# Whole rows per slot, roots in nine operations, and a new order of the first stage's lists in a routed FFN kernel

## The reference, cut to what matters

```python
# x: (128, 32, 256), 4096 tokens of 256
xc = einsum('bct,bcd->bdt', x, cond_weights[itok])        # one 32x32 matrix per batch
scores = sigmoid(xc @ gate_w.T)                            # 32 experts in 4 groups of 8
sb = scores + gate_bias
# best 2 groups by the sum of their 2 best sb, then the best 8 experts within them
wsel = scores[topi] / scores[topi].sum(-1) * 2.5           # cw: (4096, 32), zero elsewhere
x_lat = xc @ fc1_w.T                                       # 128 wide
h = relu2(x_lat @ w1[e].T) * cw[:, e]                      # relu2 is the square of relu
y_lat = sum over e of h @ w2[e].T
out = x + relu2(xc @ shared_up_w.T) @ shared_down_w.T + y_lat @ fc2_w.T
```

## Time and profile before

| | us |
|---|---|
| median of 3 runs | 442.08 |
| lowest, highest | 438.94, 444.67 |
| the profiled execution | 445.29 |
| its span, first to last instruction | 443.5 |

### The profile page before, as it was taken

The page is one execution under the profiler, slowest core; times in us unless marked ns, Lnnn a source line. Parts: engine busy times, 40 slices in busy tenths (PEclk is TensorE's granted clock), DMA queues, the critical chain, the costliest instruction groups (busy, mean ns, idle before and its releaser), DMA issues. The chain is left out here.

```text
span 443.5 us, 7029 instructions
## 1 busy us (share of the span) xinstructions
PE 397.0 (90%) x2261; PEld 345.9 (78%) x2261; DVE 307.5 (69%) x580; ACT 253.5 (57%) x330; POOL 197.5 (45%) x153
## 2 busy tenths in 40 slices
PE   8798989999989928799999999999999999999920
PEld 8788989999979828588888888888878888888810
DVE  0167997799898823697787887787767888876200
ACT  1274442734654520768778778778776787775310
POOL 5000076746776700006444576552644455434562
PEclk9899996999999968999999999999999999999555
DMA  6991473742752778858999988899998899979532
GB/s 173 251 308 41 144 289 102 239 177 72 239 220 96 223 226 257 261 181 225 210 222 234 200 214 231 222 216 315 329 351 224 231 209 304 358 221 243 111 40 31
DMA packets 66249, 93.55 MB, mean 211 GB/s; under 512 B 19295, under 2 KB 48086, under 8 KB 65622
## 3 DMA queue, kind: packets, MB, share of 16 engines
q1 hardware_dynamic: 52210, 77.71, 54.6%
q0 software_dynamic: 13296, 15.08, 20.1%
q10 hardware_dynamic: 708, 0.32, 0.3%
HBM read 94.48 MB, written 30.18 MB: 281 GB/s over the span
## 5 line engine op out<-in xcount | busy, mean ns | idle before, releaser
L530 POOL DMA_INDIRECT out_x<-res,sid_sb x70 | 122.0, 1742 | 161.9 <-DMA out_x<-res,sid_sb 72.0
L1011 DVE TENSOR_TENSOR act_lo<-act_full,act_hi 128x1024 fp32r<-128x1024 f32 (+3 forms) x92 | 105.9, 1151 | 24.7 <-ACT act_full L874 18.5
L1277 DVE SCALAR_TENSOR_TENSOR scaled<-h_banks,cond_bd 128x1024 f32<-128x1024 f32 (+3 forms) x76 | 86.5, 1138 | 42.3 <-PE h_banks L694 42.0
L694 PE MATMUL h_banks<-xc_hi,w_ring 128*128 128x512 f32 (+3 forms) x304 | 95.4, 396 | 4.0 <-DMA w_ring<-w_dram 1.8
L509 POOL DMA_INDIRECT rows_dram<-payload,slot_idx x64 | 68.6, 1072 | 56.0 <-DVE payload L1152 30.6
L715 PE MATMUL y_banks<-act_hi,w_ring 128*128 128x512 f32 (+3 forms) x304 | 79.3, 384 | 1.5 <-ACT act_hi L872 1.5
L872 ACT ACTIVATE act_hi<-scaled 128x1024 fp32r<-128x1024 f32 (+3 forms) x76 | 74.9, 986 | 2.6 <-PE y_banks L715 1.8
L874 ACT ACTIVATE act_full<-scaled 128x1024 f32<-128x1024 f32 (+3 forms) x76 | 74.7, 983 | 0.0
L715 PEld LDWEIGHTS y_banks<-act_hi,w_ring 128*128 128x128 f32 x304 | 56.7, 195 | 12.5 <-ACT act_hi L872 1.2
L694 PEld LDWEIGHTS h_banks<-xc_hi,w_ring 128*128 128x128 f32 x304 | 52.0, 193 | 16.1 <-issue 4.9
L694 PE MATMUL h_banks<-xc_lo,w_ring 128*128 128x512 f32 (+3 forms) x152 | 57.9, 381 | 0.0
(11 more groups left out here) (147 smaller groups left out, 642.3 us busy)
## 6 DMA issues: line engine op xcount, KB each, us to landing
w_ring<-w_dram SPq DMA_DIRECT2D x76, 512.0 KB
cond_bd<-s_dram SPq DMA_DIRECT2D x64, 512.0 KB, 5.5
w_dram<-w_ring SPq DMA_DIRECT2D x8, 1024.0 KB, 7.4
x_in<-in_x SPq DMA_DIRECT2D x8, 512.0 KB, 6.8
res<-in_experts_raw SPq DMA_DIRECT2D x4, 1024.0 KB, 10.2
out_x<-x_in SPq DMA_DIRECT2D x8, 512.0 KB, 3.8
rows_sb<-rows_dram SPq DMA_DIRECT2D x16, 256.0 KB, 4.8
rows_dram<-in_pad_rows SPq DMA_DIRECT2D x5, 328.0 KB, 4.3
```

Of the source, the lines that this page charges most:

```text
L530: pool.indirect_dma_start(out, bass.IndirectOffsetOnAxis(ap=sid_sb[:, i % SID_RING, j, GROUP_SIZE:PER_GROUP], axis=0), res[:, i % 2, j * H ...
L694: last = pe.matmul(h_banks[:, s, m * BANK:m * BANK + SIZE[i]], w, v, start=n == 0, stop=n == 2)
L1011: dve.tensor_tensor(lo, full, hi.bitcast(f32), ALU.subtract).then_inc(act_lo_ready, 1)
L1277: dve.scalar_tensor_tensor(pair(scaled, i, u), h, 0.0, scale, ALU.max, ALU.mult).then_inc(scaled_ready, 1)
```

## The change

- Row layout: a row is now 128 latents, 32 roots and one id (161 words for 164). SP loads a whole row per slot, `load_rows(i)` only, into a ring of eight tiles that lies in `payload`; `sid_sb`, `rows_sb` and the table's column are gone. The routing's scratch gets a tile of its own.
- ACT gets `gather_s(i)`: it copies all 32 roots of a tile's rows into `s_rows`; PE transposes 128 columns instead of 36, `store_s` writes 128 rows of 512 B instead of 36, and `load_scale` picks the group by the table.
- `roots` has nine operations: one step of second and one of third order from another start.
- `scatter` has no pauses.
- SP: `store_shared(3)` and (4) ahead of `store_split(2)`; `store_split(3)` behind the first two row loads; rows are loaded four tiles ahead.
- The lists of PE, ACT and DVE in the first stage are put in another order.

```diff
-ROW = LAT + GROUPS * PER_GROUP
+ID = LAT + EXPERTS
+ROW = ID + 1
...
             def load_rows(i):
+                row_of.append(sp.value_load(table[0:1, T_ROW + i:T_ROW + i + 1], min_val=0, max_val=DUMMY))
+                if i >= ROWS_RING:
+                    sp.wait_ge(out_added, ADDS_TO[i - ROWS_RING + 1] * DMA)
+                src = rows_dram[bass.ds(row_of[i], SIZE[i]), :].rearrange("(p j) c -> p j c", j=ROWS_OF[i])
+                sp.dma_start(tile_rows[:, i % ROWS_RING, 0:ROWS_OF[i], :], src)\
+                    .then_inc(rows_loaded[i % ROWS_RING], DMA)
...
-                src = s_dram[i % S_RING, 2 * u * SIZE[i]:(2 * u + 2) * SIZE[i]].rearrange("(a n) -> a n", a=1)
+                of_group = s_dram[i % S_RING, 0:EXPERTS * SIZE[i]].rearrange("(g n) -> g n", g=GROUPS)
+                src = of_group[bass.ds(group_of[i], 1), 2 * u * SIZE[i]:(2 * u + 2) * SIZE[i]]
...
             for u in range(PAIRS):
                 load_weights(0, u)
-            store_split(3)
             sp.wait_ge(pads_stored, GROUPS * DMA)
             sp.wait_ge(dummy_stored, DMA)
             sp.wait_ge(rows_scattered, scatters(BATCHES - 1))
-            load_sid(0)
             load_rows(0)
-            read_table(1)
-            load_sid(1)
             load_rows(1)
+            store_split(3)
             store_shared(6)
...
-                    if n == FIRST_TILE[k] + BT and k < 2:
-                        pool.wait_ge(rows_scattered, TOP_GROUPS * n * DMA)
...
+            def gather_s(i):
+                act.wait_ge(rows_loaded[i % ROWS_RING], (i // ROWS_RING + 1) * DMA)
+                if i >= 2:
+                    act.wait_ge(s_transposed, i - 1)
+                act.activation(s_rows[:, i % 2, 0:ROWS_OF[i], :], tile_rows[:, i % ROWS_RING, 0:ROWS_OF[i], LAT:ID],
+                               ACT.Copy).then_inc(s_rows_ready, 1)
...
+                c, y, q = (t[:, 0:NT[k], :] for t in (clamped, root, squared))
+                step(dve.tensor_scalar(c, cw[:, 0:NT[k], :], TINY, None, ALU.max))
+                step(dve.tensor_scalar(y.bitcast(i32), c.bitcast(i32), -0.5, INVERSE_ROOT, ALU.mult, ALU.add))
+                step(dve.tensor_tensor(q, y, y, ALU.mult))
+                step(dve.scalar_tensor_tensor(q, q, -STEP_LESS * 3 / 8, c, ALU.mult, ALU.mult))
+                step(dve.scalar_tensor_tensor(y, q, STEP_ALL * 3 / 8, y, ALU.add, ALU.mult))
+                step(dve.tensor_tensor(c, cw[:, 0:NT[k], :], y, ALU.mult))
+                step(dve.scalar_tensor_tensor(q, c, 64 / 9, y, ALU.mult, ALU.mult))
+                step(dve.scalar_tensor_tensor(q, q, -10 / 3, q, ALU.add, ALU.mult))
+                dve.scalar_tensor_tensor(payload[:, tiles_of(k), LAT:ID], q, 5.0, c, ALU.add, ALU.mult)\
+                    .then_inc(s_ready, 1)
```

More of the change, by code:

```diff
@@ L88 @@
 TABLE_CONSTS = INDEX0 + GROUPS
-T_ROW, T_GROUP, T_COL, T_NEED = (n * X_TILES for n in range(4))
-T_PAD = 4 * X_TILES
+T_ROW, T_GROUP, T_NEED = (n * X_TILES for n in range(3))
+T_PAD = 3 * X_TILES
 TABLE = T_PAD + GROUPS
@@ L132, in adaln_ffn @@
         act_lo = sb("act_lo", [P, 2, UNIT], f32r)
-        rows_sb = sb("rows_sb", [P, 2, BT, LAT])
-        sid_sb = sb("sid_sb", [P, SID_RING, BT, PER_GROUP], i32)
+        routing = sb("routing", [P, 4, NB * EXPERTS])
+        s_rows = sb("s_rows", [P, 2, BT, EXPERTS])
         s_t = sb("s_t", [P, 2, BANK])
@@ L155, in adaln_ffn @@
         biased, work, masked, left = (
-            rows_sb[:, n // 2, 2 * (n % 2):2 * (n % 2) + 2, :].rearrange("q j l -> q (j l)")
-            .rearrange("q (n e) -> q n e", e=EXPERTS) for n in range(4))
+            routing[:, n, :].rearrange("q (n e) -> q n e", e=EXPERTS) for n in range(4))
         cw, clamped, root, squared = (s_t[:, n // 2, (n % 2) * NB * EXPERTS:(n % 2 + 1) * NB * EXPERTS]
@@ L522, in _ @@
             for i in range(X_TILES):
[L523 removed]
+                pool.wait_ge(rows_loaded[i % ROWS_RING], (i // ROWS_RING + 1) * DMA)
                 if i > 0:
@@ L753, in _ @@
             project(5)
+            rank(1)
             shared_down(3)
-            rank(1)
             gate_and_latent(4)
@@ L762, in _ @@
             shared_up(6)
+            rank(2)
             shared_down(5)
-            gate_and_latent(6)
             shared_up(7)
             project(7)
-            rank(2)
+            gate_and_latent(6)
             shared_down(6)
@@ L770, in _ @@
             shared_up(8)
+            rank(3)
             shared_down(7)
-            rank(3)
             shared_up(9)
             shared_down(8)
+            rank(4)
+            count_all()
             shared_up(10)
@@ L777, in _ @@
             shared_up(11)
-            rank(4)
-            count_all()
             shared_down(10)
@@ L956, in _ @@
             square_shared(11)
-            for u in range(12, SHARED_UNITS):
-                relu_shared(u)
-                square_shared(u)
+            relu_shared(12)
+            square_shared(12)
+            relu_shared(13)
+            square_shared(13)
+            round_weights(3)
+            relu_shared(14)
+            square_shared(14)
+            relu_shared(15)
+            square_shared(15)
+            gather_s(0)
             copy_s(0)
@@ L964, in _ @@
             for i in range(1, 3):
+                gather_s(i)
                 copy_s(i)
@@ L973, in _ @@
                     round_x(i + 1)
+                if i + 3 < X_TILES:
+                    gather_s(i + 3)
                 square(i, 2)
@@ L1303, in _ @@
             slot_of_token(0)
+            combine_weights(0)
+            roots(0)
             rest_of_projection(3)
-            combine_weights(0)
             add_shared(0)
             rest_of_weights(0)
-            roots(0)
             rest(2)
@@ L1327, in _ @@
             pick_groups(2)
+            rest(6)
+            read_rank(2)
+            slot_of_token(2)
             largest(2)
             mark(2)
-            rest(6)
             add_shared(2)
@@ L1339, in _ @@
             pick_groups(3)
-            rest_of_weights(2)
-            add_shared(3)
-            rest(8)
-            read_rank(3)
-            slot_of_token(3)
             largest(3)
@@ L1348, in _ @@
             roots(3)
+            read_rank(3)
+            slot_of_token(3)
+            group_scores(4)
+            rest(8)
+            add_shared(3)
+            pick_groups(4)
+            largest(4)
+            mark(4)
             rest(9)
-            group_scores(4)
-            pick_groups(4)
-            add_shared(4)
-            rest(10)
             read_rank(4)
             slot_of_token(4)
-            largest(4)
-            mark(4)
-            rest(11)
             combine_weights(4)
             roots(4)
+            rest(10)
+            add_shared(4)
+            rest_of_weights(2)
+            rest(11)
             add_shared(5)
+            tile_table()
             rest(12)
-            tile_table()
             rest(13)
+            add_shared(6)
             rest_of_weights(3)
-            add_shared(6)
             rest(14)
```

110 lines of the change are left out of this document (36 added, 74 removed).

## The result

The changed kernel took 451.73 us (median of 4 runs, 449.19 to 453.58), the kernel before beside it 442.66 (438.94 to 444.67): a ratio of 1.0249, 95% interval 1.0183 to 1.0315. The quotient of the two medians is 1.0205; ratios here go by each kernel's fast runs, those within 1.5% of its fastest, so they can differ from that quotient (most of all for g3_mended, where two of ten runs count). The forecast was 439.2 with a range from 428 to 450. The profiled execution took 453.58 us, its span 451.7 us, 8.2 more than before.

The account below looks back on a forecast made before the run. It saw the kernel bound by the border between stages, DVE's list order in the first stage, and POOL's last adds. +3.7 us at the second stage's start and -6.5 at the end gave about -2.9, so 439.2 us, range 428 to 450.

Parts of the forecast that it names:

- Up to shared_up(6): First stage, PE: earlier rest(3) and rank(1) remove waits and the clock stays up, -5.3 us (bounds -2.0 to -5.3).
- To shared_down(8): First stage, from shared_up(6): DVE's list takes 32.0 us against PE's 27.2 of work, so PE waits, +4.8 us (0 to +6).
- To the end of shared_down(11): First stage, from shared_down(8): a 1.3 us wait for a rest behind roots(3) goes, -1.3 us (-1.3 to 0).
- tile_table ahead of rest(12): First stage, DVE: the table block delays shared_down(12), a 5.0 us PE wait, +4.4 us (+2 to +5).
- The clock: PE, first stage: of the two new waits, one counted as a fall to the low clock, +2.5 us (0 to +5).
- The border: Between stages: first scale transpose comes 3.7 us after PE's last unit instead of 7.8, -4.1 us.
- From the transpose to the experts: First scale transpose to first expert square: whole-row load of tile 2 and smaller terms, +2.7 us (0 to +5).
- The small terms of that sum: Transpose to experts: gather on ACT +0.4, one table read and issue fewer -0.7, last split meeting the scales' store +1.0 us.
- Second stage: Expert tiles: gathers, wider transposes and stores hide under PE's work, 0; without that cover 5.7 us.
- The end: Tail, POOL's adds into out: landings 0.8 us shorter over 8 tiles, -6.5 us (0 to -9).
- the two bad rivals meeting: Costlier lists (0.16) and no tail gain (0.20) together: 451.5 us; slower than 450.9 given chance 0.10.
- the rival in the prediction: Tail: adds don't land sooner, their own read and write setting the time; tail gives 0, 445.7 us, chance 0.20.

Follow-up runs that it names:

- g3_mended: Changed kernel with three moves of orders (table, rank reads, row loads) and a pause after every four tiles of scatters: 0.9701 of the kernel before, 463 kind.
- m1: Changed kernel, no pauses, rest(12) ahead of the table, rest(8) and add_shared(3) ahead of rank reads, row loads 2 and 3 earlier: 440.39 us, 0.9944, 443 kind.
- h1: Changed kernel with scales broadcast to partitions 0 to 63 alone, so outputs are not the reference's: 1.0118 of the kernel before, 443 kind.
- m2: Changed kernel with the three moves of orders and the kernel before's two pauses in the first two batches' scatters: 441.94 us, 1.0015, 443 kind.
- after_again: Changed kernel once more, nothing edited, on a chip of the 463 kind: 1.0432 of the kernel before.
- f3_pauses: Changed kernel with the pauses between the scatters of the first two batches put back: 1.0176 of the kernel before, 463 kind.
- e1: Changed kernel with rest(12) put back ahead of tile_table() in DVE's order: 1.0159 of the kernel before, 463 kind.
- e3: Changed kernel with row loads of tiles 2 and 3 right behind tile 1's on SP's queue: 1.0272 of the kernel before, 463 kind.
- g1: Changed kernel with a pause after every four tiles of scatters in all batches: 0.9991 of the kernel before, 463 kind.

## Why the prediction was wrong

By its own steps, span against span. The forecast was -2.8, the change +8.2.

- *Up to shared_up(6)*, -5.3: from shared_down(1) on -5.6, and the clock stayed up. Right. But shared_down(1) itself began 2.1 us later, behind a wait of 3.2 us and a shared_down(0) at a mean clock of 0.63 (36.96 to 41.50). The forecast had nothing for this. m1, with the same start, ran it at 36.56 in 3.10 us, so I take the 2.1 for a difference between executions; there is one profile of the changed kernel on this kind of chip.
- *To shared_down(8)*, +4.8: measured +5.4, with the 4.5 us wait on `x_in`. Right.
- *To the end of shared_down(11)*, -1.3 and with the clock's 2.5 +1.2: +1.5. Right.
- *tile_table ahead of rest(12)*, +4.4: the wait of 5.0 us came, and with the clock's price behind it the stretch took +6.2. Right.
- *The clock*, "I count one fall ... +2.5": wrong. Both new waits were followed by a stretch at the low clock, 121.0 to 126.4 at 0.50 and 153.0 to 158.1 at 0.55. The prediction had the rule of the Trainium skill before it ("TensorE: Matmul & The Clock Gate", on HAM oscillation), by which both fall; the trace agrees with it, and my middle between none and two had no ground.
- *The border*, -4.1: 164.52 to 169.84 is +5.3 on a PE that was 9.7 late, -4.4. Right, and 3.35 us of idle for 3.7.
- *From the transpose to the experts*, +2.7 (0 to +5): by the first copy of results +3.9. The cause I named, the whole-row load of tile 2 behind the weights, is the main one: in m1, where that load goes first, this stretch is only 0.5 us longer than before (35.1 for 34.6). The small terms of that sum (+0.4, -0.7, +1.0) rest on no row, and no run measured them one by one.
- *Second stage*, 0: -0.8 up to the 28th copy, with most of the gathers in it. Right.
- *The end*, "a sixth off a landing ... -6.5": this step failed, and it is the largest. A landing took 6.0 us for 5.8, and the tail 62.7 for 62.9. This is no accident of one execution: the tail took 61.4 to 68.7 us in the 14 profiles with whole rows (h1 aside) and 58.6 to 63.1 in the five with the old layout. The sign that I had named for it, a POOL wait total still near 72 us, reads 61.4 and would have misled: with the waits called "issue" the total is 104.7 us, and it was 102.2 before. The longest of the latter (in the kernel before 7.17 us, up to the add at 411.38) stand ahead of a tile's first add, where POOL waits for landings.

```profile
POOL out_x L530 <- issue: 30.2, 50, 7.2
```

Of the 11.0 us missed, 6.3 are the end, 4.6 lie ahead of the border (2.1 the start, most of the rest the second fall) and 1.2 follow it; the border and the second stage gave 1.1 back. In kind that is the case which I wrote down as the two bad rivals meeting, at 451.5, and gave a tenth. That the sum also agrees with the measured 451.73 is luck: 3.3 us of it were for a half-clock stretch near 70 us that didn't stay, and the 2.1 at the start and 1.2 at the border, which it didn't have, fill their place.

Why the end failed is settled in part. I had counted packets: 1,024 per tile became 128, and on SP's queue they did fall by 58%. h1 shows that a landing goes with the scale loads beside it, which the change left alone; the small packets weren't what an add waited for. The Trainium skill, "DMA: Bandwidth & Descriptors", section "Queues, rings and completion order", has an engine take turns between its queues by the packet. As the rival in the prediction read it, an add waits for the packet in front, now a bigger one, and not for SP's backlog; the unchanged landing came out that way. The fall to 4.3 us in h1 neither confirms nor refutes it: there the packets of SP's queue filled 34.2% of the engines' time for 56.6%, so that fewer stood in front at all. Whether bytes or the number of scale packets count wasn't separated.

The direction was wrong because a sure loss ahead of the border (+5.1, argued step by step) was set off against a guessed gain behind it. And one edit I priced at nothing on principle: the pauses. On the chip of the prediction that was nearly right; m2 against m1 gives them 0.7 points of cost, not clear of noise. On the other kind their removal is 2.5 points of loss (after_again against f3_pauses), by a mechanism that the trace before doesn't show.

Open: what makes the signals late. The rows show only that it goes with scatters under way. Nor do I know why only some chips have it, or how the gain of the three moves splits between them, on either kind; e1 and e3 were run beside no unedited copy of the changed kernel, and on the 443 kind no move was run alone. m1 and m2 weren't run on the 463 kind, nor g1 to g3 on the 443 one. And the changed kernel has one profile on the chip of the forecast, so the steps above carry the scatter of single executions.

## What to carry to other kernels

Where two engines are both nearly full, walk the second one's list and ask before each long block which operation behind it the first one waits for (here three operations moved ahead of two blocks, and two loads moved ahead on SyncE's queue, were together worth about 3%), and move the lists of all engines and the DMA queue together. A loss that is derived operation by operation shouldn't be balanced by a gain that rests on how traffic might behave. A pause in a stream of indirect DMAs that looks useless on one chip may be worth 2.5% on another, so measure on more than one, always against the kernel before on the same chip.

## What the runs showed of the hardware

- The same program took 443 us on some chips and 463 on others. On the slower ones ScalarE was released by "remote" signals 9.5 and 14.4 us after the work it waited for was done (after_again, at 72.40 and 145.68), and PE's matmuls came in groups 0.2 to 1.7 us apart (after_again, e1_table) while POOL wrote rows without a stop. From the first to the 28th copy of results both kinds took the same, 179.6 to 181.4 us in twelve profiles and 180.2 to 181.5 in seven (h1 aside).
- Such stretches shrank when no more than 8 scatters were under way: PE busy 34.58 us of 40 instead of 26.50 (g1 against after_again, on two chips), and 20.00 of 20 instead of 15.60 (f3 against after_again, on one chip). They weren't gone: g1 still has 13.6 us of "remote" waits.
- In the changed kernel waits of 3.2, 4.5 and 5.0 us were each followed by 4.5 to 5.4 us of PE at a mean clock of 0.63, 0.50 and 0.55. In m1_mends two waits of 0.9 and 1.7 us within 5 us were followed by a shared_up of 4.5 us instead of 3.0, its first 2.3 us at 0.50.
- Halving 512 KB loads on SyncE's queue took 28% off the landing of GpSimd's 19 adds beside them (6.0 to 4.3 us, changed kernel and h1).
